# adaLN attention with a routed FFN: new setup, output of the pairs by ScalarE and GpSimd, last pair's FFN in two parts, new step orders

## The reference

```python
mod = (_silu(c) @ wmod).reshape(16, 6, 1, -1)
sa, ca, ga, sb, cb, gb = ...                       # shift, scale and gate of attention and of the FFN
ga = (2 * (ga >= 0) - 1) * max(|ga|, 0.25)         # gb likewise
h = _layernorm(x) * (1 + ca) + sa
x = x + ga * attention(h)    # one head of width 256, causal, softmax of |q k| / 16
h = _layernorm(x) * (1 + cb) + sb
x = x + gb * ffn(h)
# ffn: scores of 8 clusters and of 64 tiles (h @ signatures), each put through a sigmoid and a table of
# 8 knots; first best cluster, first best tile in it; gelu(h @ w1) @ w2, tanh -> 2 numbers of a token;
# a spline of 16 terms with the chosen tile's weights -> mag;
# y = layernorm(h + mag * directions[tile]) * gamma + beta
```

## Time and profile before

| | |
|---|---|
| median of 3 runs | 471.96 us (468.45 to 473.19) |
| the profiled execution | 471.67 us, of which the span of the trace is 469.8 us |
| mean granted TensorE clock | 0.931 |
| busy, share of the span | PE 85%, DVE 85%, ACT 63%, POOL 14% |
| chain that ended last | DVE 45%, PE 42%, waiting for nothing seen 8% |

### The profile page before, as it was taken

The page is one execution under the profiler, slowest core; times in us unless marked ns, Lnnn a source line. Parts: engine busy times, 40 slices in busy tenths (PEclk is TensorE's granted clock), DMA queues, the critical chain, the costliest instruction groups (busy, mean ns, idle before and its releaser), DMA issues.

```text
span 469.8 us, 7656 instructions
## 1 busy us (share of the span) xinstructions
PE 399.8 (85%) x2072; PEld 308.7 (66%) x2072; DVE 398.5 (85%) x1367; ACT 296.5 (63%) x645; POOL 67.4 (14%) x82
## 2 busy tenths in 40 slices
PE   2697899999999999899989998999899999463330
PEld 2555578777777877687768776877677778452220
DVE  4417637387859899999999999999999899999996
ACT  2230365877698769676967697769776976651400
POOL 1002310302020002400250015001400220031040
PEclk9977899999999999999999999999999999796565
DMA  8503102101200213112310231122100210040112
GB/s 292 142 30 105 74 23 79 35 1 45 69 23 1 69 45 114 45 28 86 114 45 25 91 112 47 22 91 86 50 1 1 73 64 1 4 130 0 35 57 89
DMA packets 26234, 28.72 MB, mean 61 GB/s; under 512 B 3888, under 2 KB 21552, under 8 KB 26192
## 3 DMA queue, kind: packets, MB, share of 16 engines
q1 hardware_dynamic: 24160, 26.38, 17.8%
q10 hardware_dynamic: 2032, 1.85, 1.2%
HBM read 19.77 MB, written 8.45 MB: 60 GB/s over the span
## 4 chain that ended last, share of the span: by engine, by line
DVE 45%; PE 42%; issue 8%; ACTq 2%; ACT 2%; DVEq 0%
PE bank L511 8%; PE bank L530 8%; PE bank L490 6%; PE bank L500 6%; PE bank L553 3%; DVE y L1278 3%; DVE y L1246 3%; DVE x L1091 3%; DVE res L1288 3%; DVE st L1254 2%; DVE probs L1077 2%; DVE st L1046 2%; PE bank L520 2%; ACTq L680 2%; DVE v L1070 2%
## 5 line engine op out<-in xcount | busy, mean ns | idle before, releaser
L511 PE MATMUL bank<-h,g 128*128 128x128 f32 (+3 forms) x256 | 80.2, 444 | 4.9 <-DVE v L1070 4.9
L978 POOL TENSOR_TENSOR res<-x,gb_row 128x512 f32<-128x512 f32 x32 | 44.5, 1407 | 268.3 <-DMA out<-res 268.3
L530 PE MATMUL bank<-v,probsT 128*128 128x257 f32 x320 | 79.1, 382 | 0.0
L500 PE MATMUL bank<-m_ga,h 128*128 128x258 f32 x256 | 68.8, 394 | 5.2 <-DVE rows L1360 3.2
L530 PEld LDWEIGHTS bank<-v,probsT 128*128 128x128 f32 x320 | 57.1, 190 | 6.6 <-DVE y L1246 0.3
L490 PE MATMUL bank<-h,a_sb 128*128 128x512 f32 x128 | 60.4, 595 | 0.0
L511 PEld LDWEIGHTS bank<-h,g 128*128 128x128 f32 x256 | 44.7, 195 | 22.1 <-issue 8.5
L500 PEld LDWEIGHTS bank<-m_ga,h 128*128 128x128 f32 x256 | 47.7, 197 | 15.7 <-issue 4.3
L736 ACT ACTIVATE bank<-bank,v 128x128 f32<-128x128 f32 (+1 forms) x64 | 31.7, 495 | 41.4 <-PE bank L511 29.1
L1077 DVE CUSTOM_DVE_ANT_0 probs<-bank,cmask 128x128 f32<-128x128 f32 (+1 forms) x64 | 31.1, 485 | 23.3 <-ACT bank L736 23.3
L742 ACT ACTIVATE probs<-probs,negmax 128x128 f32<-128x128 f32 (+1 forms) x64 | 35.5, 557 | 5.9 <-DVE negmax L1077 5.9
(11 more groups left out here) (167 smaller groups left out, 770.1 us busy)
## 6 DMA issues: line engine op xcount, KB each, us to landing
x<-in_L_attn_x SPq DMA_DIRECT2D x16, 512.0 KB, 3.5
out<-res SPq DMA_DIRECT2D x16, 512.0 KB, 3.0
a_row<-gate_rows SPq DMA_DIRECT2D x16, 256.0 KB, 3.2
gb_row<-gate_rows SPq DMA_DIRECT2D x16, 256.0 KB, 3.2
wide<-in_L_wmod ACTq DMA_DIRECT2D x2, 768.0 KB, 7.6
res<-in_L_attn_Wq SPq DMA_DIRECT2D x1, 256.0 KB, 5.0
res<-in_L_attn_Wk SPq DMA_DIRECT2D x1, 256.0 KB, 7.3
res<-in_L_attn_Wo SPq DMA_DIRECT2D x1, 256.0 KB, 10.1
```

Source lines behind the costliest of these rows:

```text
L500: last = mm(ps[:, 0:VW], h[s][:, c, t * P:(t + 1) * P], m_ga[p % 2][s][:, c, :], start=(c == 0), stop=(c == KC - 1))
L511: last = mm(ps[:, 0:w], g[s][:, c, t * P:(t + 1) * P], h[s][:, c, 0:w], start=(c == 0), stop=(c == KC - 1))
L530: last = mm(ps[:, 0:D + 1], probsT[s][t][:, j * P:(j + 1) * P], v_sb[s][:, j, 0:D + 1], start=(j == 0), stop=(j == t))
L978: gp.tensor_tensor(res[:, 2 * u:2 * u + 2, :], x2[p % 2][s][:, t, :], gb_row[p % 2][s][:, 1:2, :].broadcast_to([P, 2, D]), ALU.add).then_i ...
```

## The change

Five things.

1. The last pair is two groups in the FFN, one for each sequence: groups 0 to 6 are pairs, 7 and 8 are sequences 14 and 15. Attention goes by pairs as before. There are 9 routers and splines in place of 8, the last two of half the size.
2. The output of groups 0 to 6: ACT makes `yh` (y * rstd + nmr) in place, tile by tile, GpSimd multiplies it with the gate row (`yg`, two tiles) and adds it to `res` (`yo`, two tiles). DVE has a fourth Newton instruction (`nmr`) instead of `oa` and `ob`. Groups 7 and 8 keep `oa` and `ob` on DVE.
3. Setup: silu is taken after c is turned (128x32 in place of 16x256); the gates of sequences 0 and 1 come from PE on all 128 partitions (`su_gax`), so that pair 0 doesn't wait for the way through DRAM; the router's tables are made by GpSimd (`sp_sig`, `sp_rest`) between its `ms` steps; the copies of A and of the signatures are ACT's; half of xhat and of h of sequence 0 is DVE's; the loads are put in another order and on other queues (the biases on GpSimd's, wmod in three parts).
4. The order of every engine is now three lists: filling, a repeated superstep for k = 5, 6, 7, and draining, with setup steps mixed into the filling. The superstep is another one too.
5. Another table of banks.

```diff
+        GROUPS = [(2 * p, 2 * p + 1) for p in range(PAIRS - 1)] + [(B - 2,), (B - 1,)]
+        BY_DVE = PAIRS - 1
...
+            def su_gax(b):
+                pe.wait_ge(in_mod_ga, 16)
+                pe.wait_ge(cT_rdy, 1)
+                mod_rows(free(f"su_gax{b}", (ga_own[b], 1)), 2, P,
+                         lambda c: c_T[:, c, b:b + 1].broadcast_to([P, P])).then_inc(ga_two[b], 1)
...
+            def yh(g, t):
+                act.wait_ge(ln3_ready, g + 1)
+                A(y[:, t, :], y[:, t, :], ACT.Identity, bias=ln3["nmr"][:, t:t + 1],
+                  scale=ln3["rstd"][:, t:t + 1]).then_inc(yhat_rdy, 1)
...
+            def yg(g, u):
+                pool.wait_ge(yhat_rdy, NT * before(g) + 2 * u + 2)
+                pool.wait_ge(gb_ld[g % 2][u // 2], 16 * gb_uses(g, u // 2))
+                own = y[:, 2 * u:2 * u + 2, :]
+                tt(own, own, gb_row[g % 2][u // 2][:, 0:1, :].broadcast_to([P, 2, D]), ALU.mult).then_inc(scaled_rdy, 1)
+
+            def yo(g, u):
+                pool.wait_ge(scaled_rdy, 2 * before(g) + u + 1)
+                pool.wait_ge(base_rdy, 2 * before(g) + u + 1)
+                own = res[:, 2 * u:2 * u + 2, :]
+                tt(own, own, y[:, 2 * u:2 * u + 2, :], ALU.add).then_inc(res_rdy, 2)
...
             def base(g, u):
+                need(pool, sent[u // 2], 16 * sum(1 for group in GROUPS[0:g] if u // 2 < len(group)))
...
+            for w, name in ((bq, "bq"), (bk, "bk"), (bv, "bv")):
+                gp.dma_start(w[:, :], col(ins[f"L0_attn_{name}"]), allow_slow_non_contiguous=True).then_inc(in_bias, 16)
...
+            def sd_gab(b):
+                dve.wait_ge(vb_rdy, 1)
+                dve.wait_ge(ga_own[b], 1)
+                tt(a_row[0][b][:, D:2 * D], vb_bc[:, 0:D], a_row[0][b][:, 0:D], ALU.mult).then_inc(ga_first[b], 1)
...
+            for i in range(0, 2):
+                ms(0, i)
+            sp_sig()
+            ms(1, 0)
+            sp_rest()
...
-            ffn_constants()
-
             def superstep(k):
...
-                oa(k - 5, 0)
...
-                ob(k - 5, 0)
```

More of the change, by code:

```diff
@@ new lines, in _ @@
+            S_(7, 1, 3)
+            AT(7, 1, 2)
+            for i in range(0, 2):
+                HT(7, i)
+            FS(7, 0)
+            PT_(7, 1, 3)
+            FS(7, 1)
+            AT(7, 1, 3)
+            OHT(6, 0)
+            GA(6, 0)
+            OHT(6, 1)
+            BT(6, 0)
+            for i in range(1, 3):
+                GA(6, i)
+            HD(7)
+            for i in range(3, 7):
+                GA(6, i)
+            BT(6, 1)
+            GA(6, 7)
+            CM(7)
@@ L919, in superstep @@
[L919 to L931 removed]
+                b_abs(k - 1, 1, 0)
+                c_fs(k - 2, 1)
+                c_oht(k - 3, 0)
@@ L933, in _ @@
+            c_ga(7, 3)
+            elo(8)
+            yh(6, 4)
+            gelu(8)
+            for i in range(5, 8):
+                yh(6, i)
+            tanh(8)
+            y_gs(7)
+            c_oht(8, 0)
+            for i in range(0, 4):
+                c_ga(8, i)
+            y_gs(8)
         @block.gpsimd
@@ new lines, in _ @@
+            for i in range(0, 2):
+                ms(0, i)
+            sp_sig()
+            ms(1, 0)
+            sp_rest()
+            ms(1, 1)
+            for i in range(0, 2):
+                ms(2, i)
+            ms(3, 0)
+            base(0, 0)
+            ms(3, 1)
+            ms(4, 0)
+            for i in range(1, 4):
+                base(0, i)
+            ms(4, 1)
+            yg(0, 0)
+            yo(0, 0)
+            yg(0, 1)
+            yo(0, 1)
+            base(1, 0)
+            ms(5, 0)
@@ new lines, in _ @@
+            yg(0, 2)
+            base(1, 1)
+            yo(0, 2)
+            yg(0, 3)
+            yo(0, 3)
+            for i in range(2, 4):
+                base(1, i)
+            ms(5, 1)
+            yg(1, 0)
+            yo(1, 0)
+            yg(1, 1)
+            yo(1, 1)
+            base(2, 0)
+            ms(6, 0)
+            yg(1, 2)
+            base(2, 1)
+            yo(1, 2)
+            yg(1, 3)
+            yo(1, 3)
+            for i in range(2, 4):
+                base(2, i)
@@ new lines, in _ @@
+            ms(6, 1)
+            yg(2, 0)
+            yo(2, 0)
+            yg(2, 1)
+            yo(2, 1)
+            base(3, 0)
+            ms(7, 0)
+            yg(2, 2)
+            base(3, 1)
+            yo(2, 2)
+            yg(2, 3)
+            yo(2, 3)
+            for i in range(2, 4):
+                base(3, i)
+            ms(7, 1)
+            for i in range(0, 2):
+                yg(3, i)
+            for i in range(0, 2):
+                yo(3, i)
+            yg(3, 2)
+            base(4, 0)
@@ new lines, in _ @@
+            yo(3, 2)
+            base(4, 1)
+            yg(3, 3)
+            yo(3, 3)
+            for i in range(2, 4):
+                base(4, i)
+            yg(4, 0)
+            yo(4, 0)
+            yg(4, 1)
+            yo(4, 1)
+            yg(4, 2)
+            base(5, 0)
+            yo(4, 2)
+            base(5, 1)
+            yg(4, 3)
+            yo(4, 3)
+            for i in range(2, 4):
+                base(5, i)
+            for i in range(0, 2):
+                yg(5, i)
@@ new lines, in _ @@
+            for i in range(0, 2):
+                yo(5, i)
+            yg(5, 2)
+            yo(5, 2)
+            yg(5, 3)
+            base(6, 0)
+            yo(5, 3)
+            for i in range(1, 3):
+                base(6, i)
+            yg(6, 0)
+            yo(6, 0)
+            yg(6, 1)
+            yo(6, 1)
+            yg(6, 2)
+            yo(6, 2)
+            yg(6, 3)
+            base(6, 3)
+            yo(6, 3)
+            for i in range(0, 2):
+                base(7, i)
+            for i in range(0, 2):
+                base(8, i)
```

2832 lines of the change are left out of this document (2062 added, 770 removed), and 16 rows, old and new, of the table BANK.

## The result

The changed kernel takes 525.04 us (median of 4 runs, 520.48 to 529.19), the kernel before 471.62 beside it (468.45 to 473.19): ratio 1.111, 95% interval 1.100 to 1.123.

The account below looks back on a forecast made before the run. PE was taken to bound the early part, DVE 3.7 middle periods and the draining, with both engines close. 469.8 - 9 - 4 + 2 + 2 = 460.8 us of span, forecast 462 us (456 to 467), whole range 449 to 474.

Parts of the forecast that it names:

- 36.5 + 4.8 = 41.3 us of 46, hidden as long as the period stays over 42: ACT in a middle period: 8 yh at 0.598 us add 4.8 us to its work and cost no time.
- In-order engines that are both full lose a little on each other; I take 46.4: Middle period: DVE's 45.4 and PE's 45.8 us are even, giving a period of 46.4 us, 1.1 less than now.
- DVE's sum: DVE's work in a middle period after the change: 36.4 us plus 9.0 us of being held, 45.4 us.
- its price: Middle: time each GpSimd instruction holds DVE, 0.64 us in the new order, 0.76 in the order before.
- 1.7 us a period at most: Middle: PE's 45.8 against DVE's 47.5 us limits the gain from taking work off DVE to 1.7 us a period.
- the -4 of the sum: Middle: 1.1 us less in each of 3.7 periods on DVE, -4 us.
- the ports hold more: Rival for middle and draining: GpSimd holds DVE 0.95 us per instruction, slower than before, 481 us; chance 0.12.
- the bound at 0.95 us a hold: Middle: upper bound if each GpSimd instruction holds DVE for 0.95 us, +9 us; among the rivals +8.
- Between: +2 us: Before attention's end: sequence 14's FFN puts about 2.8 us of PE work into a PE-bound stretch, +2 us.
- Setup and filling: Start of the kernel: PE reaches its first V at 34.7 us instead of going on at 48.84, -9 us.
- Draining: After attention: DVE work removed comes back as waiting for GpSimd's 24 instructions, 70 us against 68.2, +2 us.
- yh and the longer way of the output at nothing: Middle: ACT's yh hidden, output's longer route costed at nothing, up to 2 us a period if its cover is gone.

Follow-up runs that it names:

- b_id_noout: Kernel before without table loads (Identity for Gelu and Tanh), DVE's oa and ob cut to one column of 256: 462.92 us, ratio 0.984.
- a_id_pool: Changed kernel without table loads (Identity for Gelu and Tanh), GpSimd's yg and yo cut to one column of 256: 458.64 us, ratio 0.971.
- a_id: Changed kernel with Identity in place of Gelu and Tanh and no preload behind tanh, 1 table load instead of 57: 495.79 us, ratio 1.049.
- a_pool: Changed kernel with its 57 table loads, GpSimd's yg and yo cut to one column of 256: 498.89 us, ratio 1.060.
- a_id_yh: Changed kernel without table loads (Identity for Gelu and Tanh), ScalarE's yh cut to one column of 256: 493.89 us, ratio 1.046.
- b_swap_yh: Kernel before with output of pairs 0 to 6 by ScalarE and GpSimd, yh cut to one column of 256: 508.35 us, ratio 1.079.
- 5: Long GpSimd products nobody waits for, added without table loads to the changed kernel (yg, yo cut), 480.13 us, and to the kernel before, 508.46 us.
- b_swap_pool: Kernel before with output of pairs 0 to 6 by ScalarE and GpSimd, yg and yo cut to one column of 256: 478.75 us, ratio 1.016.
- b_id_dummy: Kernel before without table loads, two long GpSimd products nobody waits for added behind each base of pairs 0 to 6: 508.46 us, ratio 1.078.
- a_id_dummy: Changed kernel without table loads, yg and yo on one column, a long GpSimd product nobody waits for behind each: 480.13 us, ratio 1.017.
- a_id_dve: Changed kernel without table loads, output of all groups by DVE (oa, ob) in the new orders, yh, yg, yo removed: 493.82 us, ratio 1.047.

## Why the prediction was wrong

One ledger through the runs, in us: before without loads 469.9; output off DVE 7.0 less (b_id_noout); setup, last pair and new orders together 4.3 less (458.6, a_id_pool); yg and yo on GpSimd 37.2 more (a_id); table loads 29.2 more (the kernel after, 525.0). The last two overlap: taken out of after first, yg and yo give 26.1 us and the loads 40.3 (a_pool).

**The first step that failed: "36.5 + 4.8 = 41.3 us of 46, hidden as long as the period stays over 42".** ACT works 49.44 us in a superstep of after. I added yh and left out that the order of functions changed: 7 more table loads, 9.0 us a superstep, in front of the guesses. The order of ACT's functions and the two places that ask for a table stood in the changed program before any run; I hadn't gone through them for loads. The traces have 57 and 17. Worth 29 us of the 53 over before.

**The second: "In-order engines that are both full lose a little on each other; I take 46.4".** DVE's sum was right, 45.29 us in a_id against 45.4 forecast, and its price nearly so (0.58 us of hold for each GpSimd instruction against 0.64). What I put on top of the sum for two engines near their limit was 1 us, and it is 6.4. The new order leaves DVE these 6.4 us of idling even without yg and yo (a_id_pool), where PE's 46 us hide them. I took the holds as work that shifts into such room; they fall on instructions of the chain that ended last (273 to 282 us in a_id) and go into the period one to one. The gain on the other side was small: PE bounds the period right under DVE, as I had said myself (1.7 us a period at most), and cutting oa and ob gave 0.8. Worth 37.2 - 7.0 = 30 us, against the -4 of the sum. In the order of before the exchange costs 40 us too, so it isn't the new order that makes it dear. The rival "the ports hold more" had the sign, and the superstep as a place, but not the mechanism: the holds weren't longer, they were in the way.

Two smaller faults of the reading behind the price: 0.42 us is L1226 when it isn't held, its median is 0.876, and the instruction is held in half of the pairs; and the bound at 0.95 us a hold is +9 in one place and +8 among the rivals. Neither moves the sum.

**The third: "Between: +2 us", and the stretches that the sum left out.** The sum priced 3.7 periods of the middle, and of the last two pairs of attention only 2.8 us of PE work. Without loads and with the output cut on both sides:

| kernel | pair 0 | pair 5 | pair 7 | end of the span |
|---|---|---|---|---|
| b_id_noout | 78.3 | 306.4 | 397.4 | 458.7 |
| a_id_pool | 68.8 | 298.4 | 402.2 | 457.8 |
| a_id | 66.6 | 311.9 | 427.0 | 492.7 |

From pair 5 to pair 7 b_id_noout takes 91 us and a_id_pool 104: 13 us more where the sum had 2. PE is busy for 96.0 us there against 90.5 and stands still for 7.7 us against 0.5. About 6 us of it come back, for the draining behind it is that much shorter (55.6 against 61.3 us). Output and loads add more to each pair there than to one in the middle: yg and yo 5.7 us (a_id against a_id_pool) where pairs 1 to 5 have 3.1 each, the loads 6.9 (after against a_id) where those have 3.5. Why this stretch is so sensitive wasn't tried.

**Setup and filling: right.** The first V on PE in the kernel after, forecast for 34.7 us:

```profile
32.72 1.03 PE L562 MATMUL bank<-m_ga,h 128*128 128x258 f32 x4
```

It goes on at 35.79 us, and pair 0 ends 9.9 us earlier than before, where the sum had -9. That the two kernels with output and loads away differ by 4.3 us (458.6 and 462.9, each ratio being good to 0.6%), where the sum had -9 + 2 + 2 = -5, is in part luck: the lead is right, the 13 us of the last two pairs and the 6 us in the draining aren't.

**Draining: right in size** (67.9 us forecast 70; GpSimd busy for 30.5 us in 24 instructions, DVE for 61.7).

**yh and the longer way of the output at nothing: right for yh** (a_id_yh, b_swap_yh). For the way of yg and yo nothing points to it but the 10 us left open in 5.

**The range** ended at 474. The rival on the slower side went to 481, since I priced GpSimd only through DVE's sum.

Still open: b_swap_pool is 7 us above before though its DVE is 46 us less busy, so that something in the exchange beside GpSimd's length costs in that order. No kernel here beat the one before with the whole computation. What the runs point to, before's superstep and its last two pairs, with DVE's own output, behind the new setup (9.9 us ahead at pair 0), wasn't built.

## What to carry to other kernels

Before a step of ACT is moved, list the functions in the new order and count the table loads that the compiler puts in; a preload belongs behind each function that leaves the shared table, not behind one of them. An engine's sum of work is a floor for the period and not the period: ask of each microsecond added whether it stands on the route through the engines: in one and the same order 7.1 us of added DVE work cost 3.2 us of a superstep, and 4.6 us of being held, on the chain, cost 4.6. Price the last pairs, into which work of the draining is moved, like the others: here they held more than half of the loss. Work moved from DVE to GpSimd came back here as 0.6 to 0.8 us of held DVE for each GpSimd instruction of 128x512, however idle GpSimd was: look which DVE steps will run beside it before handing it over.

## What the hardware showed that I had not expected

A table load is 1283 ns in each of 57 cases, and the next instruction starts 1.29 us after the load (272.81 and 274.10); there is no further stop around it. The Trainium skill ("ScalarE: Activation LUTs", What ACT_TABLE_LOAD costs) has the 1283 ns and adds a drain of about 1380 ns; no row here shows that drain, and here the measurement decides.

GpSimd's hold on DVE is the same for a product that has nothing to do with DVE's data: 0.76 us of 1.14 when DVE is never idle (b_id_dummy). In the order of after a product of 1.06 us costs 0.38 us of the kernel's time (a_id_dummy), and a yg or yo of 1.36 us 0.66 (a_id).

The PE clock takes part. In the supersteps above in which PE rests for 3.8 to 7.6 us the mean granted clock is 0.94 to 0.97, so a part of them passes at the lower of its two levels (1.2 and 2.4 GHz); in those in which it rests for 1.0 to 1.6 us it is 1.00. The same matmuls take 47.9 to 48.6 and 46.0 to 46.1 us. More rest doesn't mean less clock in every case: 7.6 us go with 0.97 (after), 5.0 us with 0.94 (b_id_dummy), and the superstep of a_id_dve rests for 3.7 us at 1.00. Where the clock falls, about 2 us more of matmuls come on top of the waits.
